# A four-layer transformer block on one core: the experts' slot table built by one-hot products instead of indirect scatters, expert weights requested in another order

## The reference, cut to what matters

```python
logits = (x @ gate_w.T).astype(jnp.float32)
probs = jax.nn.softmax(logits, axis=-1)
topk_p, topk_i = jax.lax.top_k(probs, TOP_K)          # 8 of 64
topk_p = topk_p / jnp.sum(topk_p, axis=-1, keepdims=True)
flat_e = topk_i.reshape(-1)
onehot = jax.nn.one_hot(flat_e, NUM_EXPERTS, dtype=jnp.int32)
pos_all = jnp.cumsum(onehot, axis=0) - 1
pos = jnp.take_along_axis(pos_all, flat_e[:, None], axis=1)[:, 0]
dispatch = dispatch.at[flat_e, pos].set(x_rep, mode='drop')   # CAPACITY = 64
g = jax.nn.silu(jnp.einsum('ech,eih->eci', dispatch, w_gate))
u = jnp.einsum('ech,eih->eci', dispatch, w_up)
y = jnp.einsum('eci,ehi->ech', g * u, w_down)
out = (y_tok * w[:, None]).reshape(T, TOPK, H).sum(axis=1)
```

## Time and profile before

| | us |
|---|---|
| median of 3 runs | 2958.66 |
| fastest, slowest | 2944.38, 2959.12 |
| span of the profiled execution | 3039.9 |
| of it layer 0 and the wait for the table, to the first gather | 608.4 |
| of it experts, to the next block's first instruction | 123.1 |

### The profile page before, as it was taken

One profiled execution on the slowest core, in us unless ns is written; L12 is line 12 of the kernel. 1 busy time (PEld: TensorE's weight loads), 2 busy tenths in 40 slices (PEclk: granted clock), 3 DMA queues, 4 the chain that ended last, 5 costly groups with the idle time before them and its releaser, 6 DMA issues. The chain is left out here.

```text
span 3039.9 us, 35372 instructions
## 1 busy us (share of the span) xinstructions
PE 2503.2 (82%) x12480; PEld 1340.4 (44%) x12480; DVE 1813.2 (60%) x4051; ACT 1170.0 (38%) x2095; POOL 787.7 (26%) x494
## 2 busy tenths in 40 slices
PE   6895966186687969979989988989997998997997
PEld 2341323132354534545554454555463555454554
DVE  5663744214787747357748447776736785835775
ACT  1431422022233415236635325654415563513662
POOL 1004033462000004114414204432302442401441
PEclk8987976588587879999999999999998999999998
DMA  7411002587420020034430024432012443002443
GB/s 230 120 36 16 15 14 75 162 259 252 153 76 7 8 98 1 3 110 118 106 101 37 8 85 104 114 95 77 8 70 77 113 115 100 1 11 93 120 119 76
DMA packets 113984, 257.07 MB, mean 85 GB/s; under 512 B 37223, under 2 KB 57319, under 8 KB 107787
## 3 DMA queue, kind: packets, MB, share of 16 engines
q1 hardware_dynamic: 93978, 220.26, 24.1%
q10 hardware_dynamic: 12656, 25.97, 3.5%
q0 software_dynamic: 7168, 8.50, 1.0%
HBM read 119.81 MB, written 29.74 MB: 49 GB/s over the span
## 5 line engine op out<-in xcount | busy, mean ns | idle before, releaser
L857 POOL TENSOR_SCALAR pbuf<-pbuf,recip 128x1024 f32<-128x1024 f32 x128 | 364.7, 2849 | 947.2 <-DVE recip L761 947.2
L806 ACT ACTIVATE pbuf<-ps,least 128x1024 f32<-128x1024 f32 x256 | 284.3, 1113 | 297.6 <-DVE least L754 221.8
L754 DVE CUSTOM_DVE_ANT_0 ps<-ps,mask 128x1024 f32<-128x1024 f32 x256 | 308.0, 1245 | 138.7 <-PE ps L686 137.6
L583 POOL TENSOR_SCALAR pbuf<-pbuf,recip 128x512 f32<-128x512 f32 x128 | 200.4, 1577 | 459.6 <-DVE recip L504 459.6
L686 PE MATMUL ps<-kH,qT 64*128 64x512 f32 x1024 | 269.9, 648 | 50.0 <-ACT pbuf L806 47.2
L711 PE MATMUL ps<-work,vh 128*64 128x256 f32 x2048 | 250.3, 388 | 0.0
L554 ACT ACTIVATE pbuf<-ps,least 128x512 f32<-128x512 f32 x256 | 172.7, 686 | 156.3 <-DVE least L494 156.3
L1505 ACT ACTIVATE early<-ps 128x1536 f32<-128x1536 f32 x86 | 124.0, 1441 | 273.1 <-PE ps L1338 199.9
L768 DVE STREAM_TRANSPOSE pbuf<-pbuf 128x2048 f32<-128x2048 f32 (+1 forms) x128 | 226.3, 1769 | 0.8 <-issue 0.8
L1578 DVE TENSOR_REDUCE mh<-ps 128x3 f32<-128x1536 f32 x86 | 150.0, 1745 | 117.0 <-PE ps L1327 63.7
L991 POOL DMA_INDIRECT slot_token<-info,place x128 | 125.9, 984 | 238.6 <-DVE info L1743 191.3
(11 more groups left out here) (343 smaller groups left out, 4110.6 us busy)
## 6 DMA issues: line engine op xcount, KB each, us to landing
work<-pbuf SPq DMA_DIRECT2D x784, 96.0 KB, 2.5
work<-pbuf ACTq DMA_DIRECT2D x240, 96.0 KB, 2.9
early<-in_L_wgu SPq DMA_DIRECT2D x22, 768.0 KB
expert_rows<-zero_rows SPq DMA_DIRECT2D x16, 1024.0 KB, 11.6
yg<-expert_rows SPq DMA_DIRECT2D x16, 1024.0 KB, 5.9
early<-in_L_wd SPq DMA_DIRECT2D x22, 384.0 KB
arena<-in_L_wo SPq DMA_DIRECT2D x8, 1024.0 KB, 9.0
arena<-in_L_wff SPq DMA_DIRECT2D x4, 2048.0 KB, 9.3
```

Of the source, the lines that this page charges most:

```text
L583: nc.gpsimd.tensor_scalar(x, x, recip[:, n % 8:n % 8 + 1], None, mult).then_inc(probs_ready[1], 1)
L754: nc.vector.tensor_tensor_reduce(out=x, in0=x, in1=mask, scale=1.0, scalar=FMAX, op0=add, op1=ALU.min, accum_out=least[:, n % 8:n % 8 + 1])\
L806: nc.scalar.activation(to, x, ACT.Exp, bias=least[:, n % 8:n % 8 + 1], scale=-1.0, accum_out=sums[:, n % 8:n % 8 + 1]).then_inc(taken, 1)
L857: nc.gpsimd.tensor_scalar(unit(n), unit(n), recip[:, n % 8:n % 8 + 1], None, mult).then_inc(pool_divided, 1)
```

## The change

- DVE no longer makes `key`, `place8` and `info8`, and POOL's `scatter` is gone, with the table in DRAM and its load back.
- DVE makes, for each batch, `vals`: for every token and pair of experts ten bfloat16 columns (tile number, row in the tile, rank among the token's eight for each of two experts, and the weight of each split into three parts). Then, for each of 8 half tiles (128 tokens by 32 experts), `mark` compares the token's position with 0 to 63 and writes a one-hot matrix of 128 x 2048 bfloat16.
- PE multiplies them: 16 products for each half tile, one for each pair of experts, with the one-hot block as the stationary operand (128 x 128) and 10 moving columns. That is 128 products a batch. DVE adds the result to the table `slots` in SBUF (`keep_table`), 8 additions for batches 0 to 2, 4 larger ones for batch 3.
- After batch 3 DVE forms the table `taken` in SBUF with ten small instructions; POOL gathers from it directly.
- SP asks for all 9 early pairs at `av_done`, ahead of the stores of batch 3's rows. The last 5 are asked for at the head of `experts`, as before.
- The quantisation of `w3` is no longer at the head of `experts`: its DVE steps stand between pairs 4 and 11, its products (`scale_rows`) before the last two pairs' down products, and its three copies before the last two pairs' rows.

```diff
-    def scatter(b, tiles):
-        for t in tiles:
-            for k in range(TOPK):
...
-                nc.gpsimd.indirect_dma_start(
-                    taken_d[:, :], bass.IndirectOffsetOnAxis(place8[:, b % 2, t, k:k + 1], 0), info8[:, b % 2, t, k, :], None,
...
+            for i in range(HALVES if b < B - 1 else NT):
+                at["table", b, i] = int(t) + (47.6 + i if b < 2 else 47.6 + 1.5 * i if b == 2 else 50 + 0.1 * i)
...
+        def mark(b, i):
+            t, h = divmod(i, 2)
+            mine = slot[:, t, h * E // 2:(h + 1) * E // 2].unsqueeze(2).broadcast_to([P, E // 2, CAP])
+            every = slot_no[:, :].unsqueeze(1).broadcast_to([P, E // 2, CAP])
+            return nc.vector.tensor_tensor(onehot[:, i % OH, :, :], mine, every, ALU.is_equal)
...
-                        for i in range(AT_ONCE):
+                        for i in range(EARLY):
                             load_pair(sp, a, pair_weights(early, i), i, early_in[i])
...
-                sp.wait_ge(placed, 2 * B - 1)
-                for i in range(AT_ONCE, EARLY):
-                    load_pair(sp, a, pair_weights(early, i), i, early_in[i])
...
+                def table(b):
+                    for i in range(HALVES):
...
+                        pe.wait_ge(onehot_ready, HALVES * b + i + 1)
+                        for j in range(PAIRS // 2):
+                            last = nc.tensor.matmul(by_pair(k)[:, h * whole * PAIRS // 2 + j, :],
+                                                    onehot[:, i % OH, 2 * j:2 * j + 2, :].rearrange("p e s -> p (e s)"),
+                                                    vals[:, t, h * PAIRS // 2 + j, :], start=True, stop=True)
...
+                    for i in range(HALVES):
+                        yield max(t0 + 45.6, at["table", b, i] - 1.3) if b < B - 1 else t0 + 46 + 0.01 * i
...
+                        free_onehot(v, b, i)
+                        mark(b, i).then_inc(onehot_ready, 1)
...
+                        nc.vector.tensor_tensor(mine, mine, by_pair(k), add).then_inc(job_kept, 1)
...
-                scatter(B - 1, range(NT // 2, NT))
-                pool.wait_ge(taken_in, 16)
...
+                def scale_rows():
+                    pe.wait_ge(w3_ready, 1)
+                    pe.wait_ge(xgT_ready, PAIRS)
...
                     if n >= 2:
                         rows(n - 2)
+                    if n >= QUANTISED:
+                        next(steps, None)
```

More of the change, by code:

```diff
@@ L1095, in layer0 @@
         ex = keep("ex", [P, NT, E])
[L1096 to L1097 removed]
+        slot = keep("slot", [P, NT, E])
         before = keep("before", [P, NT + 1, E])
@@ L1100, in layer0 @@
         e8 = keep("e8", [P, NT, TOPK])
-        k8 = keep("k8", [P, NT, TOPK])
-        w8s = [info8.bitcast(F32)[:, i, :, :, 1] for i in range(2)]
-        off8 = keep("off8", [P, NT, TOPK])
         negm = keep("negm", [P, NT])
@@ L1566, in opening @@
                     nc.vector.memset(zero_rows[:, :], 0.0).then_inc(fill_ready, 1)
-                    for i, value in enumerate((TOK * TOPK, 0, TOK)):
-                        nc.vector.memset(no_token[:, :, i:i + 1], value).then_inc(fill_ready, 1)
+                    link(nc.vector.memset(slots[:, :, :], 0.0))
+                    for t in range(NT):
+                        nc.vector.memset(vals[:, t, :, 0], float(t + 1))
+                    v.wait_ge(consts_in, 16)
+                    v.wait_ge(fill_ready, 1)
+                    nc.vector.tensor_tensor_scan(slot_no[:, :], ones[:, 0:CAP], zero_rows[:, 0:CAP], -AWAY - 1, add, add)
                     v.wait_ge(gates_ready, 1)
@@ new lines, in route @@
+                        nc.vector.tensor_copy(vals[:, :, :, 1].rearrange("p t j -> p (t j)"), token_f[:, 0:1].broadcast_to([P, NT * PAIRS]))
+                    else:
+                        nc.vector.tensor_scalar(vals[:, :, :, 0], vals[:, :, :, 0], float(NT), None, add)
+                    nc.vector.tensor_copy(column(0), by_expert(rep))
+                    link(nc.vector.tensor_copy(column(1), by_expert(ex)))
+                    link(nc.vector.tensor_tensor(by_expert(lg), by_expert(ex), column(1), subtract))
@@ new lines, in route @@
+                    if b < B - 1:
+                        return
+                    yield t0 + 52
+                    v.wait_ge(job_kept, nth["table", b, NT - 1] + 1)
+                    nc.vector.tensor_scalar(empty[:, :], slots[:, :, 0], 0.0, float(TOK + P), ALU.is_equal, mult)
+                    link(nc.vector.scalar_tensor_tensor(out=token[:, :], in0=slots[:, :, 0], scalar=float(P), in1=slots[:, :, 1], op0=mult, op1=add))
+                    for e in range(2):
+                        mine, at_e = slice(e * CAP, (e + 1) * CAP), 2 + 4 * e
+                        last = nc.vector.tensor_tensor(slots[mine, :, at_e + 1], slots[mine, :, at_e + 1], slots[mine, :, at_e + 2], add)
@@ new lines, in route @@
+                    link(nc.vector.scalar_tensor_tensor(out=token[:, :], in0=token[:, :], scalar=float(-P), in1=empty[:, :], op0=add, op1=add))
+                    for e in range(2):
+                        mine, at_e = slice(e * CAP, (e + 1) * CAP), 2 + 4 * e
+                        nc.vector.scalar_tensor_tensor(out=taken[mine, :, 0], in0=token[mine, :], scalar=float(TOPK), in1=slots[mine, :, at_e],
+                                                       op0=mult, op1=add)
+                        nc.vector.tensor_tensor(taken.bitcast(F32)[mine, :, 1], slots[mine, :, at_e + 1], slots[mine, :, at_e + 3], add)
```

190 lines of the change are left out of this document (94 added, 96 removed).

## The result

The changed kernel took 2994.97 us (2986.93 to 3003.67) where the kernel before took 2957.93: a ratio of 1.0144, 95% interval 1.0110 to 1.0178. It is slower; the forecast was 2967, with the range ending at 2992. A second measurement gave 1.0144 again (1.0105 to 1.0182). The profiled execution of the changed kernel has a span of 2985.2 us, where 2985 was forecast from the span before: the time is 28 us over its forecast, and the span is on it. The reason is the first thing that the runs showed.

The account below looks back on a forecast made before the run. Layer 0 was taken as PE-bound with three holes, absent from timed runs. 2958.7 + 22 (batches 0 and 1) + 8 (batch 2) - 31.6 (batch 3) + 10.5 (experts) = 2967.6, forecast 2967 us, range 2898 to 2992.

Parts of the forecast that it names:

- the holes: Layer 0 beside POOL's scatters: idle time no instruction releases, 54 to 57 us in the trace, 0 in the metric, an effect of recording.
- Rival A: The idle times at the scatters are real in timed runs too: 2907 us in the metric, chance 0.32.
- The 81.2 us: Profiled execution 3039.9 us against median 2958.66; the excess taken as a sign that timed runs lack the idle times.
- Batches 0 and 1: Tables made between layer 0's attention steps: +11.1 us a batch, +22 together, with a table step of 4.7 us.
- T: PE's time for a table's 16 small products, not in the trace: taken as 1.7 us, bounds 1.15 and 2.9.
- Batch 2: Its 8 tables among the last steps of batch 3's attention and output projections: +8 us, bounds 3 to 15.
- batch 3: From its positions to the first gather: 61.7 us before, 30.1 after without POOL's scatters, so -31.6.
- The experts: Less time ahead for loading weights, so the transfer becomes the bound: 127 us against about 116.5 in timed runs, +10.5.
- rival C: The experts' weights aren't late and the experts keep their time: 2957 us, or 2952 with faster small products; chance 0.16.
- The asks: SP asks for 9 weight pairs at `av_done`, not 4, ahead of batch 3's row stores: 0, with 30 us of cover.
- Rival B: PE's small products in the tables cost 2.9 us for 16, not 1.7: 29 us more, 2996 us; chance 0.18.
- The span of 2985: Profiled execution after the change: 3039.9 - 52 - 3 = 2985 us, with the idle times at the scatters gone.

## Why the prediction was wrong, point by point

- **What bounds the kernel, and the holes.** The holes were read rightly out of the earlier trace rows, and it was right that the metric would not gain from their going. The reason was wrong. They are not there or gone with the recording. Of the four chips of the experiments one took 3022.6 to 3044.8 us in all 17 of its timings of the kernel before, and waits without a releaser stand in all four traces taken there; none of the eleven taken on the others has one. That it is the chip, and not a state that it was in for a time, is not shown: these four kernels ran one after the other. Rival A was true on that chip (0.9854 for the changed kernel in all but the order of the asks) and false where the change was measured. The 81.2 us between the profiled execution and the median were the sign. The Trainium skill's page "NOTIFIC — the notification-queue block" (section 7.1) says that a full record queue can stall the engine that writes to it. No run here shows whether that is the cause, and why one chip has the waits and three have not it does not tell. Why is open.
- **Batches 0 and 1, the step that failed.** "8 steps cost 8 x 1.7 = 13.6" and the sum of +11.1 a batch took PE's step as its work plus T. T was 0.56, not 1.7, since the products start 26 ns apart ((0.56 - 0.168) / 15), so this term was three times too large, and DVE set the plain steps at 4.1 us. Two terms were missing. The first is a wait: the job behind a table waits for DVE's addition, which stands behind a one-hot matrix. I had asked what hides each row, not who waits behind it, though the order of DVE in the front shows `onehot0` ahead of `slots0` in every step. These waits are 13.2 us over both batches, and all of PE's idle time grew by 18. By itself that fits: new products and waits are 27 us, against 22 forecast. The second made 54 us of it: the clock, which no term of the sum had, +27 by PE's busy time (36 by the upper estimate). The waits and the clock are not two causes: with the waits cut by one swap of rows, 26 of the clock's 27 us were gone.
- **Batch 2** +8, measured +5.7 (+5.6 in the second trace of the changed kernel, +10.8 with the addition first), and **batch 3** -31.6, measured -34.3: right, batch 3 from durations of rows of similar form, batch 2 from the middle of its bounds.
- **The experts** +10.5, measured +10.2: right, and with the mechanism named there; both ends were put 2 us too short (118.6 and 128.8 us, not 116.5 and 127). So rival C, weights that aren't late, falls. The move of `w3`'s work was not run by itself; its cost lies somewhere in these 10 us. The gain of an earlier table goes back to the weights, since `more` is memory of the next block and cannot be filled before it.
- **The asks**: 0 forecast. In the kernel before nothing shows in the stages where they act; in the changed kernel the times show no difference, and the 9 us in the experts stay open.
- **Rival B** got its time right (2996) by a mechanism that was not there: T was lower, not higher, than forecast. That is no support for it.
- **The span of 2985**, which came true, was luck: holes were under-counted (the last maxima but one are at 466.1 before and at 390.8 without holes: 75 us, and up to batch 3's positions, 546.7 against 451.9, it is 95, not 54 to 57), and the tables by about as much (36). The clock has a part in the first too: it was 0.69 in the 15 us behind the first hole.

## What to carry to other kernels

When a change adds short waits to a busy TensorE, price them with the clock: look at the granted clock of the stretch, and ask for each new instruction which job of PE stands behind its last step in the order. The order of two rows on another engine was worth 0.5% here (1.0144 to 1.0091), without any change of work. And a profile whose span doesn't fit the timed runs is a profile of something else: take it again before building on it.

## What the runs showed of the hardware that I had not expected

- Sixteen bfloat16 products with 128 x 128 stationary operands and 10 moving columns take 0.56 us, one every 26 ns, though each loads new weights.
- On one chip of four that timed the kernel before, waits without a releaser of up to 32 us stand beside POOL's indirect DMAs, and the kernel takes 3% more. Without the scatters in layer 0 they stand only in the experts, beside the gathers, and are at most 5 us. In the maxima's case only TensorE's signal was missing; which unit held it no run shows.
- Where most gathered rows are the same row and most result rows are not stored, full DMA engines moved 225 GB/s, where filled tables leave 321. The two were not tried apart.
